# Changing the order of VectorE's work inside a slot of an attention layer, and where TensorE spreads the softmax sums

## What is computed

```python
def _L0_attn_ref(x, qkv_w, proj_w, proj_b, slopes):
    qkv = (x @ qkv_w.T).reshape(B, N, 3, H, D).transpose(2, 0, 3, 1, 4)
    q, k, v = (qkv[0], qkv[1], qkv[2])
    ...
    q = q * cos + _rotate_half(q) * sin
    k = k * cos + _rotate_half(k) * sin
    attn = jnp.einsum('bhqd,bhkd->bhqk', q, k) * SCALE
    ...
    attn = attn + alibi[None]
    w = jax.nn.softmax(attn, axis=-1)
    out = jnp.einsum('bhqk,bhkd->bhqd', w, v)
    out = out.transpose(0, 2, 1, 3).reshape(B, N, C)
    return out @ proj_w.T + proj_b
...
x = x + _L0_attn_ref(_layernorm(x, axis=-1), L0_attn_qkv_w, L0_attn_proj_w, L0_attn_proj_b, L0_attn_slopes)
x = x + _L0_ffn_ref(_layernorm(x, axis=-1), L0_ffn_W, L0_ffn_b, L0_ffn_V_r, L0_ffn_C)
```

## Time and profile before

| | us |
|---|---|
| median of 3 runs | 2271.48 (2270.88 to 2272.22) |
| the profiled execution, its own time | 2274.01 |
| span of the profile | 2272.7 |
| TensorE busy | 2140.8 |
| VectorE busy | 1980.0 |
| ScalarE busy | 1383.4 |
| GpSimd busy | 1151.2 |

### The profile page before, as it was taken

How to read it: one execution, slowest core, us unless ns; L and a number is a source line. 1 busy time by engine, 2 the same in 40 slices (tenths; PEclk the granted TensorE clock), 3 DMA queues, 4 the chain that set the end, 5 groups by cost and what they waited for, 6 DMA issues and landing times. The chain is left out here.

```text
span 2272.7 us, 77397 instructions
## 1 busy us (share of the span) xinstructions
PE 2140.8 (94%) x31524; PEld 1130.2 (50%) x31524; DVE 1980.0 (87%) x5949; ACT 1383.4 (61%) x1666; POOL 1151.2 (51%) x966
## 2 busy tenths in 40 slices
PE   3899999999999999999999999999999999999996
PEld 1245555555555555555545555555555555555553
DVE  5599999999998989999989999998999999999972
ACT  0166666666666666666666666666666666666662
POOL 3436555554545545555555455555545555554421
PEclk8699999999999999999999999999999999999997
DMA  5323433333333332343333333333333333323310
GB/s 117 110 77 87 117 84 106 110 85 99 105 107 87 105 108 77 105 115 87 102 111 85 99 105 110 86 107 114 85 100 105 108 87 106 115 79 104 97 32 24
DMA packets 158868, 218.49 MB, mean 96 GB/s; under 512 B 19024, under 2 KB 104912, under 8 KB 158512
## 3 DMA queue, kind: packets, MB, share of 16 engines
q1 hardware_dynamic: 157232, 211.44, 32.9%
q10 hardware_dynamic: 1280, 2.10, 0.3%
HBM read 36.52 MB, written 16.78 MB: 23 GB/s over the span
## 5 line engine op out<-in xcount | busy, mean ns | idle before, releaser
L529 DVE CUSTOM_DVE_ANT_0 junk<-ps_s,alibi 128x512 bf16<-128x512 f32 x2048 | 1323.5, 683 | 191.7 <-PE ps_s L364 155.3
L673 ACT ACTIVATE pt<-ps_t 128x1024 f32<-128x1024 f32 x1024 | 1050.8, 1026 | 606.1 <-DVE ps_t L539 601.0
L364 PE MATMUL ps_s<-at 64*128 64x512 f32 x2048 | 817.5, 462 | 20.6 <-DVE row_max L529 9.7
L372 PE MATMUL ps_t<-at 64*128 64x512 f32 x2048 | 776.3, 453 | 1.2 <-ACT pt L673 1.2
L385 PE MATMUL ps_o<-pt,v_one 128*17 128x128 f32 x16384 | 642.5, 275 | 2.9
L385 PEld LDWEIGHTS ps_o<-pt,v_one 128*17 128x17 f32 x16384 | 424.0, 98 | 328.3 <-issue 220.7
L539 DVE SCALAR_TENSOR_TENSOR ps_t<-diag,slope,ps_t 128x256 f32<-128x256 f32 x1024 | 495.4, 484 | 27.6 <-PE ps_t L372 27.6
L364 PEld LDWEIGHTS ps_s<-at 64*128 64x128 f32 x2048 | 331.4, 186 | 294.2 <-DVE row_max L529 215.3
L802 POOL TENSOR_TENSOR rope_a<-rope_a,swapped 128x512 f32<-128x512 f32 x128 | 161.6, 1284 | 469.5 <-DMA swapped<-rope_b 469.5
L372 PEld LDWEIGHTS ps_t<-at 64*128 64x128 f32 x2048 | 326.4, 185 | 33.2 <-ACT pt L673 26.0
L335 PE MATMUL ps_misc<-xt,wqkv_t 128*32 128x512 f32 x2048 | 279.6, 620 | 13.8 <-DVE x L563 6.0
(11 more groups left out here) (72 smaller groups left out, 1447.8 us busy)
## 6 DMA issues: line engine op xcount, KB each, us to landing
at<-halves SPq DMA_DIRECT2D x192, 512.0 KB, 5.1
swapped<-rope_b SPq DMA_DIRECT2D x256, 128.0 KB, 2.6
x_in<-in_L_attn_x_dram SPq DMA_DIRECT2D x32, 512.0 KB, 3.9
num<-o_sb SPq DMA_DIRECT2D x512, 32.0 KB, 2.0
x_res<-in_L_attn_x_dram SPq DMA_DIRECT2D x32, 512.0 KB, 4.2
out_dram<-x_hat SPq DMA_DIRECT2D x32, 512.0 KB, 5.9
at<-spread_den SPq DMA_DIRECT2D x60, 64.0 KB
at<-max_t ACTq DMA_DIRECT2D x128, 16.0 KB
```

The source lines that it names most:

```text
L364: pe.matmul(ps_s[:, t % 2, :], operand(n, 0)[:, t * P:(t + 1) * P], operand(n, 1), start=True, stop=True).then_inc(s_done, 1)
L372: pe.matmul(ps_t[:, j, :], operand(n, 1)[:, j * P:(j + 1) * P], operand(n, 0), start=True, stop=True).then_inc(t_done, 1)
L529: dve.tensor_tensor_reduce(junk[:, t % 2, :], ps_s[:, t % 2, :], alibi[:, off:off + N], 1.0, LOWEST, ALU.add, ALU.max, row_max[:, hb % 2, ...
L673: act.activation(pt[:, h % 2, 2 * pair:2 * pair + 2, :], ps_t[:, 2 * pair:2 * pair + 2, :], ACT.Exp).then_inc(exp_done, 1)
```

## The change

In the tensor program the spreading of the softmax sums stands ahead of PV instead of behind it, in both halves of slot 15. In the vector program the diagonal goes behind the division and the additions, so that a half's order is maxima, division or additions, diagonal, statistics, reciprocals. And the statistics are taken one token tile in a half instead of two: for `x1` in slots 3 and 4, both halves each (before: two in the first half of each slot, the aggregate in the first half of slot 4), for `x_in` in slots 12 and 13, both halves each (before: two in each half of slot 13). The wait for the load of `x_in` moves to slot 12 with the first of them.

```diff
@@ tensor_program
+                    b = batch_at(slot, 31)
+                    if b is not None:
+                        spread_denominators(b, half)
                     if nv is not None:
                         weighted_values(nv, 2 * half)
                         weighted_values(nv, 2 * half + 1)
-                    b = batch_at(slot, 31)
-                    if b is not None:
-                        spread_denominators(b, half)
@@ vector_program
                         row_maximum(n, 2 * half)
                         row_maximum(n, 2 * half + 1)
-                    if nt is not None:
-                        diagonal_bias(nt, half)
                     b = batch_at(slot, 31)
                     if b is not None:
                         divide(b, half)
@@
                             add_linear("proj", b, u, x1, x_res, res_biased, x1_done)
-                        b = batch_at(slot, 35 + u)
-                        if b is not None and half == 0:
-                            dve.wait_ge(x1_done, 2 * b + u + 1)
-                            ln_stats(b, x1, 1, bn_done2, (2 * u, 2 * u + 1))
-                        if b is not None and half == 0 and u == 1:
-                            ln_mean_var(b, 1, bn_done2, aggr_done2)
                         b = batch_at(slot, 41 + u)
                         if b is not None and half == 1:
                             add_linear("ffn", b, u, y, y, x1_biased, y_done)
-                    b = batch_at(slot, -19)
-                    if b:
-                        if half == 0:
-                            dve.wait_ge(x_loaded, 16 * (b + 1))
-                            ln_stats(b, x_in, 0, bn_done, (0, 1))
-                        else:
-                            ln_stats(b, x_in, 0, bn_done, (2, 3))
-                            ln_mean_var(b, 0, bn_done, aggr_done)
+                    if nt is not None:
+                        diagonal_bias(nt, half)
+                    for u in range(2):
+                        b = batch_at(slot, 35 + u)
+                        if b is not None:
+                            t = 2 * u + half
+                            if half == 0:
+                                dve.wait_ge(x1_done, 2 * b + u + 1)
+                            ln_stats(b, x1, 1, bn_done2, (t,))
+                            if t == T - 1:
+                                ln_mean_var(b, 1, bn_done2, aggr_done2)
+                    for u in range(2):
+                        b = batch_at(slot, -20 + u)
+                        if b:
+                            t = 2 * u + half
+                            if t == 0:
+                                dve.wait_ge(x_loaded, 16 * (b + 1))
+                            ln_stats(b, x_in, 0, bn_done, (t,))
+                            if t == T - 1:
+                                ln_mean_var(b, 0, bn_done, aggr_done)
```

## The result

The changed kernel takes **2350.4 us** (median of 4, 2347.4 to 2353.7) against 2271.2 (2270.6 to 2272.2): 1.035 times as long, 95% interval 1.033 to 1.037. The forecast was 2347, in a range of 2290 to 2362. The profile has a span of 2352.3 us against 2272.7.

What follows compares the result with a forecast made beforehand. TensorE (94% busy) and VectorE (87%) were taken to bound the kernel in turns. From the profiled 2274.0 us: +50 (aggregate's wait) -14 (ffn additions) -10 (slots 12 to 15) +50 (clock) = 2350, less 2.5: 2347 us, range 2290 to 2362.

Steps and rivals of the forecast that it cites:

- The aggregate of x1: Slot 6: aggregate 1.59 us later, so TensorE waits that much longer for `x_hat2`; 48 us plus 2 in the tail, +50 us.
- The clock: Behind slot 6's longer wait (2.0 us), TensorE's clock falls to 1.2 GHz in nearly every batch; +50 us, bounds 0 and 69.
- The ffn additions: Additions ahead of the diagonal free the bank before TensorE asks; 0.24 us for each of two a batch, -14 us.
- The proj additions: Slots 2 and 3: TensorE gets its bank sooner but then waits for VectorE's maxima; 0, or another -14 us if wrong.
- Slots 12 to 15: VectorE reaches the reciprocals 0.5 us sooner, partly lost to the `den` transfer and TensorE; 0.34 us a batch, -10 us.
- Both paybacks: Slots 12 to 15's gain shrinks: PV now follows the spreading, and exponentials come late behind the second division (0.2 us at PE).
- The tail: Program's end: the last batch's statistics come one at a time after its last addition, about 2 us.
- The rival of starved exponentials: Division ahead of the diagonal starves ScalarE; exponentials hold PE 0.2 to 0.5 us in six halves, 20 to 50 us; no chance given.
- the rival by which the kernel becomes faster: Slot 6: the later aggregate is covered if VectorE's stretch held hidden bank waits; only gains stay, 2247 us; 6%.

## Why the prediction was right

It was right in size and by its main steps, the longer wait and the clock behind it. That the total came so near is partly luck: the clock measured 5 us below its term, the wait, the tail and slots 12 to 15 some 11 above theirs together.

- **The aggregate of x1.** Expected 1.59 us a batch, measured 1.6 to 1.67, and the wait total 70 against 71.6 us. The aggregate came 1.64 us later, as VectorE's work without idle time said. Undoing this part alone took the loss away, doing it alone brought it.
- **The clock.** Expected 50 us, measured 45 by the distances in the profile (18 x 1.5 + 7 x 2.6) and as much in the steady part by filling the wait; the 52 us of the whole program hold some 7 of its end. The prediction's 0.45 us lost for each us at low clock is a little high by its own rows, (1.11 - 0.63) / 1.11 = 0.43. "In nearly every batch" was 25 of 30. The price per fall was 1.5 to 2.6 us (1.67 expected as a mean over batches, 1.5 measured); the durations of 3.4 us, and twice that in some batches, were as estimated. In the Trainium skill (TensorE: Matmul & The Clock Gate, "Why this matters for your kernels") only longer idle gaps than these 2.0 us are warned of. The trace disagrees, with falls behind 25 of 30 such waits.
- **The ffn additions.** 0.24 us for each of two halves, as expected: 2.34 to 2.10 us, 14 us in all. The proj additions gave nothing, as expected.
- **Slots 12 to 15.** Mis-sized: expected 0.34 us a batch, measured 0.14. By halves, slot 14 gains 0.31 us (4.71 to 4.40) and slot 0 gains 0.32 (4.06 to 3.74), but the first half of slot 15 loses 0.49 (2.29 to 2.78), where PE now waits 0.4 us for the second reciprocal. Both paybacks were named, this one and the late exponentials (0.18 us in the second half of slot 0); the netting was too kind. Putting the spreading back behind PV does not win it back, so its position alone is not the fault. The transfer of `den` caught VectorE in 16 or 17 batches, as expected in kind.
- **The tail.** Mis-sized: about 2 us expected. From slot 6 of the last batch with scores to the end it is 129.8 us against 121.4; that batch's own stall and fall take 3.1 of the 8.4 us (9.04 against 5.97 to the middle of slot 7), so about 5 are the tail's. Behind that batch the profile has 48 us at clock 0.50, before 37.5. So most of the 5 us is likely the clock's, not the late statistics'; this was not separated.
- **The sum**: +50 (wait), +45 (clock in the 30 batches), +5 (tail), -14, -4: 82 us, with 79 measured.

The rival of starved exponentials fell as a cause (the order alone is 0.4% faster), though PE does wait for them in slot 0; the rival by which the kernel becomes faster had its price right (2247 expected, 2252 with the wait's growth undone) but not its condition.

## To carry to other kernels

When a statistic or any small step feeds a chain on another engine, count back from the consumer: if the consumer already waits, even by 0.4 us, a later start is paid in full (here 1.64 us later, 1.6 us longer), while the engine that does the step looks better balanced. Smoothing an engine's load by moving work later is only free where nobody waits for the result; here it gained 8 us for `x_in` alone and cost 99 us for `x1`. And price a longer TensorE wait twice, once as time and once as the clock behind it.

## What the chip showed

- A wait of 2.0 us on TensorE, in a stretch of light work (PE busy 1.54 of the 3.4 us before one fall, and 1.41 of 3.4 in a batch that held), was followed by a granted clock of 0.50 (1.2 GHz) in 25 of 30 batches, for 3.4 or 6.8 us, which began between 1.2 us before the wait's end and 1.5 us behind it; in the other 5 the same wait at the same place left it at 1.00. Why those held isn't settled by these runs.
- Eight products of 0.25 us each, whose result is thrown away, kept the clock at 1.00 in 28 of 30 batches and were worth 52 us in 2350.
- The clock also fell without a wait of 2.0 us: in two kernels PE had waited 0.89 and 1.06 us for a maximum in slot 5 and was busy 2.52 and 2.43 of the 3.4 us before the fall.
- A wait of 0.4 us in the same place (the kernel before) never brought it down in the steady part.
